# Cross attention with a routed FFN: the two q tiles turned by VectorE become neighbours and return through DRAM as one block

## The reference

```python
qh = softmax(einsum('bcn,oc->bon', layernorm(x), Wq) per head, over its 64) * SCALE
kh = softmax(einsum('bcn,oc->bon', ctx, Wk), over n)
vh = einsum('bcn,oc->bon', ctx, Wv)
context = einsum('bhdn,bhen->bhde', kh, vh)
out = einsum('bhde,bhdn->bhen', context, qh)
out = einsum('bcn,oc->bon', out, Wo) + bo
x = x + out / norm(out over channels) * g * sqrt(C)
```

## Time and profile before

| | us |
|---|---|
| median of 3 runs | 677.22 (676.03 to 680.52) |
| the profiled execution | 677.15 |
| its span in the trace | 675.3 |
| TensorE busy | 649.6 (96%) |
| VectorE busy | 563.3 (83%) |
| ScalarE busy | 421.8 (62%) |
| GpSimd busy | 409.7 (61%) |

### The profile page before, as it was taken

One profiled execution on the slowest core, in us unless ns is written; L12 is line 12 of the kernel. 1 busy time (PEld: TensorE's weight loads), 2 busy tenths in 40 slices (PEclk: granted clock), 3 DMA queues, 4 the chain that ended last, 5 costly groups with the idle time before them and its releaser, 6 DMA issues.

```text
span 675.3 us, 11559 instructions
## 1 busy us (share of the span) xinstructions
PE 649.6 (96%) x3718; PEld 575.1 (85%) x3718; DVE 563.3 (83%) x721; ACT 421.8 (62%) x864; POOL 409.7 (61%) x421
## 2 busy tenths in 40 slices
PE   4989999999999999999999999999999999999896
PEld 3768898988888989898988989898988899999574
DVE  5989897979797988989797979797977854666897
ACT  5555656665756666666665757575666456675784
POOL 4944375766667676676757676666656463541295
PEclk9999999999999999999999999999999999999999
DMA  8944667565766565656565666565548240000056
GB/s 297 228 126 137 196 167 206 157 193 159 199 166 189 155 195 160 192 156 191 159 192 158 189 163 190 157 186 159 167 125 232 103 131 0 1 2 0 12 214 273
DMA packets 75051, 106.12 MB, mean 157 GB/s; under 512 B 12672, under 2 KB 61344, under 8 KB 74736
## 3 DMA queue, kind: packets, MB, share of 16 engines
q1 hardware_dynamic: 73952, 101.63, 50.7%
q0 software_dynamic: 896, 2.45, 1.2%
q10 hardware_dynamic: 144, 1.31, 0.5%
HBM read 46.62 MB, written 25.17 MB: 106 GB/s over the span
## 4 chain that ended last, share of the span: by engine, by line
PE 88%; DVE 3%; DMA 3%; SPq 2%; issue 2%; ACT 1%; POOL 0%; DVEq 0%; ACTq 0%; POOLq 0%
PE ob L565 25%; PE gm L535 16%; PE gm L622 4%; PE q_slot L493 4%; PE q_slot L495 4%; PE k_slot L493 4%; PE q_slot L494 4%; PE k_slot L495 4%; PE k_slot L494 4%; PE turn L519 4%; PE turn L622 4%; PE gm L544 2%; PE turn L577 2%; SPq L404 2%; DMA x_all<-Wvd_cols 1%
## 5 line engine op out<-in xcount | busy, mean ns | idle before, releaser
L1059 POOL TENSOR_TENSOR qs_sb<-qs_sb,qrec 128x1024 f32<-128x1024 f32 x64 | 121.8, 1903 | 137.4 <-DVE qrec L1249 137.4
L565 PE MATMUL ob<-mt_sb,q_hd 128*128 128x128 f32 x1024 | 187.3, 336 | 1.5 <-issue 1.0
L565 PEld LDWEIGHTS ob<-mt_sb,q_hd 128*128 128x128 f32 x1024 | 182.8, 260 | 6.0 <-issue 4.5
L806 ACT ACTIVATE ek<-k_slot,nkm 128x1024 f32<-128x1024 f32 x62 | 69.1, 1114 | 95.2 <-DVE nkm L1213 95.0
L535 PE MATMUL gm<-ekT,ctxT 128*128 128x256 f32 x512 | 118.7, 380 | 1.7 <-issue 0.8
L1213 DVE TENSOR_REDUCE nkm<-k_slot 128x1 f32<-128x1024 f32 x62 | 74.3, 1198 | 49.2 <-PE k_slot L495 49.2
L535 PEld LDWEIGHTS gm<-ekT,ctxT 128*128 128x128 f32 x512 | 96.6, 190 | 18.1 <-issue 2.9
L816 ACT ACTIVATE qs_sb<-qs_sb 128x1024 f32<-128x1024 f32 x64 | 67.9, 1061 | 36.0 <-DVE qs_sb L1238 35.2
L1238 DVE TENSOR_TENSOR qs_sb<-q_slot,qm 128x1024 f32<-128x1024 f32 x64 | 78.4, 1224 | 2.2
L1245 DVE TENSOR_REDUCE qsum<-qs_sb 128x16 f32<-128x1024 f32 x64 | 77.0, 1203 | 3.8 <-ACT qs_sb L816 3.8
L1220 DVE STREAM_TRANSPOSE kt<-ek 128x1024 f32<-128x1024 f32 x64 | 79.0, 1234 | 0.0
(11 more groups left out here) (208 smaller groups left out, 1282.6 us busy)
## 6 DMA issues: line engine op xcount, KB each, us to landing
ekT<-kt SPq DMA_DIRECT2D x496, 64.0 KB, 2.1
q_turned<-qt SPq DMA_DIRECT2D x32, 512.0 KB, 2.9
q_hd<-q_turned SPq DMA_DIRECT2D x128, 128.0 KB, 3.1
ctx_in<-ctx_rows SPq DMA_DIRECT2D x16, 512.0 KB, 5.5
x_all<-x SPq DMA_DIRECT2D x16, 512.0 KB, 5.3
ctxT<-ctx_cols SPq DMA_DIRECT2D x16, 512.0 KB, 4.2
out<-q_hd SPq DMA_DIRECT2D x15, 512.0 KB, 2.6
Wuq_in<-Wuq_cols ACTq DMA_DIRECT2D x1, 1280.0 KB, 6.7
```

Source lines behind the costliest of these rows:

```text
L565: last = nc.tensor.matmul(ob[:, (j % 4) * C:(j % 4 + 1) * C], q, mt_sb[:, b % 2, t, :], start=(t == 0), stop=(t == T - 1))
L806: nc.scalar.activation(ek[:, i % 2, :], k_psum(b, i)[:, :], ACT.Exp, bias=nkm[:, i:i + 1], accum_out=ksum[:, b % 2, i:i + 1]).then_inc(k_e ...
L1059: nc.gpsimd.tensor_tensor(e, e, qrec[:, i % 2, :].unsqueeze(2).broadcast_to([P, PAIR, DH]), ALU.mult).then_inc(q_mul, 1)
```

## The change

The tiles that VectorE turns are 0 and 1 in place of 1 and 3, so TensorE turns 2 and 3, in steps 0 and 1. `qt` is filled by two block turns as one tile of quadrants, `(q t i n x)`, with contiguous runs of 32 floats, and contiguous input. One write of 1 MB (`q_out(b)`) waits for both turns, one set of four reads of 256 KB (`q_in(b)`, contiguous pieces of 2 KB) brings both tiles; they stand in the queue where those of tile 1 stood, and those of tile 3 fall away. One semaphore counts the reads, and both `o_pair(b, 0)` and `o_pair(b, 1)` wait for all of them. The stationary operands are contiguous, `(n t x)`, and the columns of `o_turn` are reordered to match. The wait for the weights in `stage` goes from ScalarE to SP, at the first `q_in`.

```diff
--- before.py
+++ after.py
@@ -24,7 +24,7 @@
 BLK = 32
 QUAD = P // BLK
 MOVED = 16 * QUAD * QUAD
-BY_BLOCKS = (1, 3)
+BY_BLOCKS = (0, 1)
 BY_PE = tuple(i for i in range(4) if i not in BY_BLOCKS)
 RESIDUAL_BY_VECTOR = B - 3
 LN_EPS = 1e-5
@@ -127,7 +127,7 @@
         att.close()
 
 
-        q_turned = nc.dram_tensor("q_turned", (2, len(BY_BLOCKS), P, QUAD, 2 * T * BLK), F32, kind="Internal").ap()
+        q_turned = nc.dram_tensor("q_turned", (2, P, QUAD, T * P), F32, kind="Internal").ap()
 
         stage = q_hd[:, :, :].rearrange("p t n -> p (t n)")
         WqT_in, WkT_in = stage[:, 0:HD], stage[:, HD:2 * HD]
@@ -296,8 +296,8 @@
         q_T = sem("q_T")
         q_copied = sem("q_copied")
         q_blocks = sem("q_blocks")
-        q_written = [sem(f"q_written{i}") for i in BY_BLOCKS]
-        q_back = [sem(f"q_back{i}") for i in BY_BLOCKS]
+        q_written = sem("q_written")
+        q_back = sem("q_back")
         o_back = sem("o_back")
         mean2_done = sem("mean2_done")
         nm2_done = sem("nm2_done")
@@ -405,21 +405,24 @@
                                      kt[a * BLK:(a + 1) * BLK, 2 * half:2 * half + 2,
                                         q * J * BLK:(q + 1) * J * BLK]).then_inc(k_moved[half], 16)
 
-            def q_out(b, i):
-
-                n = BY_BLOCKS.index(i)
-                sp.wait_ge(q_blocks, len(BY_BLOCKS) * b + n + 1)
-                wait(sp, q_back[n], 16 * QUAD * (b - 1))
-                sp.dma_start(q_turned[b % 2, n].rearrange("p q x -> p (q x)"), qt[:, n, :]).then_inc(q_written[n], 16)
-
-            def q_in(b, i):
-
-                n = BY_BLOCKS.index(i)
-                sp.wait_ge(q_written[n], 16 * (b + 1))
-                wait(sp, o_prod, 4 * (b - 1) + i + 1)
+            def q_out(b):
+
+                sp.wait_ge(q_blocks, 2 * b + 2)
+                wait(sp, q_back, 16 * QUAD * (b - 1))
+                sp.dma_start(q_turned[b % 2].rearrange("p q x -> p (q x)"),
+                             qt[:, :, :].rearrange("p i x -> p (i x)")).then_inc(q_written, 16)
+
+            def q_in(b):
+
+                if b == 0:
+                    sp.wait_ge(k_weights, 2)
+                    sp.wait_ge(q_weights, 2)
+                    sp.wait_ge(u_prod, 1)
+                sp.wait_ge(q_written, 16 * (b + 1))
+                wait(sp, o_prod, 4 * (b - 1) + 2)
                 for q in range(QUAD):
-                    sp.dma_start(q_hd[q * BLK:(q + 1) * BLK, i, :].rearrange("r (a x) -> r a x", a=QUAD),
-                                 q_turned[b % 2, n, :, q, :].rearrange("(a r) x -> r a x", a=QUAD)).then_inc(q_back[n], 16)
+                    sp.dma_start(q_hd[q * BLK:(q + 1) * BLK, 0:2, :].rearrange("r i (a x) -> r (i a) x", a=2),
+                                 q_turned[b % 2, :, q, :].rearrange("(a r) x -> r a x", a=QUAD)).then_inc(q_back, 16)
 
             def ffn_tables():
                 for half in range(2):
@@ -453,26 +456,18 @@
                     load_x(b + 1)
                 if has(b):
                     move_k(b, 0)
-                for i in (0, 1):
-                    if i in BY_BLOCKS and has(b - 1):
-                        q_out(b - 1, i)
+                if has(b - 1):
+                    q_out(b - 1)
                 if 2 <= b < B:
                     load_ctxT(b)
                 if 2 <= b + 2 < B:
                     load_ctx(b + 2)
-                for i in (0, 1):
-                    if i in BY_BLOCKS and has(b - 1):
-                        q_in(b - 1, i)
+                if has(b - 1):
+                    q_in(b - 1)
                 if has(b):
                     move_k(b, 1)
                 else:
                     ffn_tables()
-                for i in (2, 3):
-                    if i in BY_BLOCKS and has(b - 1):
-                        q_out(b - 1, i)
-                for i in (2, 3):
-                    if i in BY_BLOCKS and has(b - 1):
-                        q_in(b - 1, i)
 
             for b in range(B - BY_VECTOR):
                 sp.wait_ge(y_ready, b + 1)
@@ -547,7 +542,7 @@
 
             def o_pair(b, i):
                 if i in BY_BLOCKS:
-                    pe.wait_ge(q_back[BY_BLOCKS.index(i)], 16 * QUAD * (b + 1))
+                    pe.wait_ge(q_back, 16 * QUAD * (b + 1))
                 else:
                     pe.wait_ge(q_copied, turned_by_pe(b, i))
                 if i == 0:
@@ -557,7 +552,7 @@
                 if i % 2 == 0:
                     wait(pe, o_copied, 2 * b + i // 2)
                 by_pe = q_hd[:, i, :].rearrange("p (t n x) -> p t n x", t=T, n=2)
-                by_blocks = q_hd[:, i, :].rearrange("p (n x t) -> p t n x", t=T, n=2)
+                by_blocks = q_hd[:, i, :].rearrange("p (n t x) -> p t n x", t=T, n=2)
                 for n in range(2):
                     j = 2 * i + n
                     for t in range(T):
@@ -569,11 +564,10 @@
             def o_turn(b):
                 pe.wait_ge(o_scaled, b + 1)
                 for j in range(J):
-                    tile = turn[:, (j // 2) * 2 * P:(j // 2 + 1) * 2 * P]
                     if j // 2 in BY_BLOCKS:
-                        cols = tile.rearrange("p (n h a x) -> p h a n x", n=2, h=2, a=2)[:, j % 2, :, :, :]
+                        cols = turn[:, 0:QUAD * P].rearrange("p (m a x) -> p a m x", m=QUAD, a=QUAD)[:, j, :, :]
                     else:
-                        cols = tile[:, (j % 2) * P:(j % 2 + 1) * P]
+                        cols = turn[:, j * P:(j + 1) * P]
                     last = nc.tensor.transpose(cols, o_sb[:, b % 2, j, :], ident[:, :])
                 last.then_inc(o_T, 1)
 
@@ -932,9 +926,6 @@
                         ctx_high(b + 1)
                     qb, qi = (p, i - 2) if i >= 2 else (o, i + 2)
                     if has(qb) and qi in BY_PE:
-                        if qb == 0 and qi == BY_PE[0]:
-                            act.wait_ge(k_weights, 2)
-                            act.wait_ge(q_weights, 2)
                         q_copy(qb, qi)
                     if i == 0 and has(e):
                         o_square(e, 1)
@@ -1252,9 +1243,12 @@
 
                 n = BY_BLOCKS.index(i)
                 dve.wait_ge(q_mul, 4 * b + i + 1)
-                wait(dve, q_written[n], 16 * b)
-                V.transpose(qt[:, n, :].rearrange("p (m x t) -> p m t x", m=QUAD * 2, t=T),
-                            qs_sb[:, i % 2, :].rearrange("p (m q x) -> p q m x", q=QUAD, m=2 * T)).then_inc(q_blocks, 1)
+                wait(dve, q_written, 16 * b)
+                turned = qt[:, :, :].rearrange("p i x -> p (i x)").rearrange("p (q t i n x) -> p i n t q x", q=QUAD, t=T,
+                                                                             i=2, n=2)
+                V.transpose(turned[:, n, :, :, :, :],
+                            qs_sb[:, i % 2, :].rearrange("p (n t q x) -> p n t q x", n=2, t=T,
+                                                         q=QUAD)).then_inc(q_blocks, 1)
 
             def residual(b):
                 dve.wait_ge(o_T, b + 1)
```

## The result

The changed kernel takes **761.63 us** (median of 4 runs, 760.86 to 765.37), the kernel before 676.62 beside it (4 runs, 675.52 to 680.52): a ratio of 1.126, 95% interval 1.120 to 1.132. Forecast were 694 us and at most 715. The direction was right, the size was not: 85 us lost instead of 17. The profiled execution took 765.37 us, its span 763.6.

The account below looks back on a forecast made before the run. TensorE was taken to bound the kernel (88% of the chain). A 4.9 us wait outweighs the 3.99 us gain: periods of 33.9 instead of 32.81 add 13 us, the ends 4, giving 694 us; range 668 to 715.

Parts of the forecast that it names:

- the ends: First and last stretches outside the twelve steady periods: 1.4 us lost at the start, 2.8 at the end, together 4.
- Stationary operands: TensorE's output products of tiles 3 and 1: contiguous reading takes 3.93 and 3.62 us to 1.78, 3.99 us a period.
- The rule weighed against this term: Skill's weight-load time by number of columns alone; by it the gain from contiguous stationary operands would be nought.
- Block turns: VectorE's turn of a q tile: 1.23 us instead of 2.04, still tied to step 3's first k product (T).
- The new wait: TensorE ahead of tile 0's products waits 4.9 us for the whole block, there at T + 16.1; period 33.9 us.
- Read issued to the last landing: Four reads of the block on SP's queue: 5.3 us plus 1.24 for the doubled size, at 320 GB/s.
- Write issued to read issued: Landing of the block's 1 MB write on SP's queue: 4.3 us taken, 4.9 as the other end.
- The clock in the wait: Rival, chance 0.20: tile 0's products at half speed behind the wait, 1.8 us a period; 701 us, or 715 in all twelve.
- The periods behind them carry fewer context loads; I count those unchanged: Periods behind the twelve steady ones, with fewer context loads: no change in their time counted.
- The upper bound: Top of the whole kernel's range, 715 us; the range was to hold 8 in 10 from 668.
- its long end, 711 us: Whole time with write 4.9 and read 5.3 + 2.04 us: block there at T + 17.5.

Follow-up runs that it names:

- experiments 6 and 8: First: changed kernel with tiles 2 and 3 as VectorE's neighbours, 711.93 us. Second: kernel before with reads inside the k move, alone 678.37, with operand step two 657.71, one 663.75.
- Experiment 7: Kernel before with the operands of tiles 1 and 3 read contiguously from the unchanged layout, transfers and order kept (output differs); 670.73 us.
- experiments 3 and 4: Changed kernel with DRAM laid out by quadrant, 764.91 us; then without quadrant exchange: one whole-row read 706.46, one read of 2 KB pieces 738.57, four 128-partition reads 739.90.
- experiment 1: Changed kernel with the two context loads issued ahead of the block's write instead of between write and read; 766.25 us.
- experiment 5: Changed kernel with overwritten identity products added ahead of TensorE's two waits, so that it has work until the block is there; 745.51 us.
- experiment 8's first kernel: Kernel before with only SP's order changed: each read of turned q behind the first four DMAs of the next k move; 678.37 us.

## Why the prediction was wrong

The mechanism is the one forecast; the write and the read came out longer, the clock that was priced as a rival came nearly in full, and the ends cost six times what was counted. All figures a period are means of the twelve.

Right:
- *Stationary operands*: 3.93 and 3.62 became 1.78 at full clock; only behind the small products of m, where 3.93 stood, a contiguous group takes 1.98 (experiments 6 and 8), 0.2 less gained there than the prediction took. Experiment 7 reads the same operands contiguously and finds 1.78 in its chain. The rule weighed against this term (the Trainium skill, TensorE: Matmul & The Clock Gate, LDWEIGHTS (loading the stationary operand)), time by columns alone, holds here for steps of one and two floats and not for four.
- *Block turns*: 1.23 taken, 1.19 measured; the turn did stay tied to T (T + 3.98 against T + 3.97).
- *The new wait*: its place, the order of its path, and that it spends more than the gain. From T + 18.3 to the next T it is 17.81 and 1.85, the part of the clock and of the start behind a wait.

Wrong, by size:
- *"Read issued to the last landing", 6.54*, measured 8.18 in the rows and 7.93 in the mean: 1.4 us a period, 17 us in twelve. The step that failed is the rate of 320 GB/s taken between "Pieces of 1 KB came at 257 GB/s, of 4 KB at 382". Those two rows differ in the size of their pieces, but also in the partitions that they fill: the slower was the read of a turned tile, 32 partitions at a time, the faster a context load into 128. The difference was put down to the pieces, so the larger pieces were promised a rate that came, in the runs, with more partitions in one transfer (about 300 GB/s against 190 to 230). Four reads of 128 partitions take 6.8 us, near the forecast; the same four of 32 partitions take 7.8 (experiments 3 and 4). The reason given for the length of the read before, the context loads ahead of it, is worth at most 0.8 us in the changed kernel (experiment 1); in the kernel before it was not tried.
- *"Write issued to read issued", 4.3*, measured 4.86: 0.56 a period, 7 us. Both ends were in the text, 4.3 from the median of 32 writes and 4.9 from the write at this place; half of those 32 belong to tile 3 and have no context loads behind them, so the row of the place was the better one.
- *The clock in the wait*, a rival at 0.20, priced at 1.8 us: from tile 0's products to the next write 25.06 us pass instead of 23.04, 2.0 a period and 24 us in twelve; experiment 5 gives 1.65 of the 2.0 to the clock, and most of the rest is the start behind a wait (2.05 for 1.78). The lower clock stands behind tile 0's wait in all twelve periods, at least in part. The only row for it was the run-out at the end, where the clock fell 3.7 us after work stopped, and the forecast's wait was 4.9; the text called it open and gave it one chance in five. The 0.20 was too low, and the waits that came were not the one forecast but two, 2.09 and 3.15 us in the rows.
- *"The periods behind them carry fewer context loads; I count those unchanged"*, and the ends: 4.2 us forecast for all of them, 27 measured. The path closes on itself in those periods as in any other, and the context loads were not what made it long, so nothing was cheaper there; the last read but one even took 10.3 us, in a period in which ScalarE's queue issues a load of 1280 KB of FFN weights just ahead of it.

The sum: 17 forecast, and 17 + 7 + 24 + 23 (27 less 4) more make 88, as between the spans. The upper bound failed because its long end, 711 us, held a slow write and read without the clock, and 715 the clock without them; both came. Even the two together, some 733, stay short: the read was longer than its own long end (5.3 + 2.04 = 7.34), and the ends were counted at 4 us.

## What to carry to other kernels

A round trip through DRAM that has slack when each tile travels alone loses it when two tiles travel together: the first then waits for the second, and its landings become TensorE's wait, with the clock's price on top. Before a DMA rate is carried from one row to another, compare the partitions that the two transfers fill, not only their pieces; here the engines moved 190 to 230 GB/s in reads that fill 32 partitions each, about 300 in reads of 128 with the same pieces. A layout change that frees one engine should be tried first without its transfer and with the queue's order looked over: here a step of two floats, the reads inside the k move and an early context load give 6%, where the full rearrangement lost 13%.

## What was not expected

- A stationary operand with a step of two floats is read about as fast as a contiguous one (1.88 against 1.78 us for sixteen records), one with a step of four at half the speed (3.62).
- The length of a wait does not by itself tell the clock behind it. In experiment 7 the g sums behind a wait of 2.46 us run at the full clock and behind one of 2.43 at the lower one (granted clock 0.50 at 343); in experiment 6 products behind waits of 2.75 us went either way. In the changed kernel the first of the two waits, 2.0 to 2.1 us, left the g sums at the full clock in four of the twelve periods. What decides was not tried.

```profile
309.74 1.97 PE L535 MATMUL gm<-ekT,ctxT 128*128 128x256 f32 x8 [2.46 <-issue]
...
342.21 3.56 PE L535 MATMUL gm<-ekT,ctxT 128*128 128x256 f32 x8 [2.43 <-issue]
```

- The write of the turned tiles gets slower when the loads are put ahead of it (by 0.5 us in the mean) by about what the read gains (0.4): the order within the group of transfers shifts the cost between them.
- Pieces of 256 B on the read (3.0 us to landing) cost little against 512 B (2.7) or 1 KB (2.8 in experiment 8's first kernel) as long as the place hides them.
